# Rotary attention on one core: two half sums of a group's first numerator stack with one score between them instead of two

## The reference

```
q_rot = einsum('bhci,cij->bhcj', q, R);  k_rot = einsum('bhci,cij->bhcj', k, R)
attn_num = exp(einsum('bhqd,bhkd->bhqk', q_rot, k_rot) / scale)
attn_den = exp(einsum('bhqd,bhkd->bhqk', q, k) / scale)
attn_den = sum(attn_den, axis=-1, keepdims=True)
attn = where(causal == 0, 0.0, attn_num / attn_den)
y = einsum('bhqk,bhkd->bhqd', attn, v)
```

## Time and profile before

| | |
|---|---|
| median of 3 runs | 1891.65 us (1891.63 to 1892.13) |
| profiled execution | 1890.58 us |
| its span (first to last instruction) | 1888.6 us |
| TensorE busy | 1632.1 us (86%) |
| ScalarE busy | 1442.5 us (76%) |
| VectorE busy | 1193.2 us (63%) |
| mean granted clock of TensorE | 0.963 |

### The profile page before, as it was taken

How to read it: one execution, slowest core, us unless ns; L and a number is a source line. 1 busy time by engine, 2 the same in 40 slices (tenths; PEclk the granted TensorE clock), 3 DMA queues, 4 the chain that set the end, 5 groups by cost and what they waited for, 6 DMA issues and landing times. The chain is left out here.

```text
span 1888.6 us, 33689 instructions
## 1 busy us (share of the span) xinstructions
PE 1632.1 (86%) x12879; PEld 628.3 (33%) x12964; DVE 1193.2 (63%) x2130; ACT 1442.5 (76%) x2508; POOL 315.0 (17%) x420
## 2 busy tenths in 40 slices
PE   5799999999999999864888888989888888883995
PEld 3222222222222222241333332433343333222674
DVE  7999989999999999887454636454545423223220
ACT  4477777777777778725999999999989999991321
POOL 4500010010001001032000100010001032312466
PEclk9799999999999999977999999999999999996998
DMA  5311111111111110004111211122111222232333
GB/s 169 98 39 38 38 44 38 39 44 38 38 38 44 38 39 20 8 25 157 50 43 44 93 51 51 60 71 89 51 51 63 89 85 89 95 115 66 117 57 30
DMA packets 70960, 115.86 MB, mean 61 GB/s; under 512 B 10041, under 2 KB 55973, under 8 KB 66192
## 3 DMA queue, kind: packets, MB, share of 16 engines
q1 hardware_dynamic: 59536, 92.88, 15.6%
q0 software_dynamic: 11264, 20.83, 4.0%
HBM read 71.49 MB, written 42.14 MB: 60 GB/s over the span
## 5 line engine op out<-in xcount | busy, mean ns | idle before, releaser
L786 ACT ACTIVATE rows_and_probs<-psS 128x512 f32<-128x512 f32 x1010 | 549.1, 596 | 166.7 <-PE psS L684 166.0
L808 DVE TENSOR_REDUCE max_of_halves<-psM 128x2 f32<-128x1024 f32 x512 | 623.9, 1225 | 54.6 <-PE psM L647 20.5
L1647 ACT ACTIVATE exps<-cpsS 128x1024 bf16<-128x1024 f32 x512 | 546.3, 1109 | 22.7 <-PE cpsS L1389 22.1
L1389 PE MATMUL cpsS<-rotary_stack 128*128 128x512 bf16 x959 | 288.1, 385 | 77.6 <-ACT exps L1647 30.5
L704 PE MATMUL psO<-rows_and_probs,plain_v 128*9 128x256 f32 x4096 | 317.6, 382 | 5.3 <-ACT rows_and_probs L786 0.6
L1657 ACT ACTIVATE cprobs<-cpsS 128x1024 f32<-128x1024 f32 x256 | 281.7, 1100 | 21.6 <-PE cpsO L1422 18.9
L1369 PE MATMUL cpsS<-rotary_stack 128*128 128x512 bf16 (+3 forms) x748 | 188.5, 327 | 54.1 <-ACT exps L1647 35.5
L647 PE MATMUL psM<-plain_top 64*128 64x512 bf16 x1024 | 205.9, 384 | 20.6 <-DVE max_of_halves L808 20.2
L684 PE MATMUL psS<-plain_top 64*128 64x512 bf16 x1010 | 208.4, 388 | 0.0
L684 PE MATMUL psS<-plain_rest 64*128 64x512 bf16 x1010 | 202.6, 378 | 0.0
L1422 PE MATMUL cpsO<-cprobs,rotary_v 128*9 128x512 f32 (+3 forms) x1536 | 153.7, 488 | 0.8 <-DVE rotary_sums L1981 0.8
(11 more groups left out here) (301 smaller groups left out, 1756.1 us busy)
## 6 DMA issues: line engine op xcount, KB each, us to landing
rotary_stack<-q_parts SPq DMA_DIRECT2D x48, 192.0 KB
rotary_stack<-k_parts SPq DMA_DIRECT2D x48, 192.0 KB
rotary_stack<-q_rot_parts SPq DMA_DIRECT2D x48, 192.0 KB
rotary_stack<-k_rot_parts SPq DMA_DIRECT2D x48, 192.0 KB
tokens_taken<-parts_and_sums POOLq DMA_DIRECT2D x32, 259.0 KB, 4.2
plain_top<-q_parts SPq DMA_DIRECT2D x64, 96.0 KB
plain_top<-k_parts SPq DMA_DIRECT2D x64, 96.0 KB
e_x<-tokens_taken SPq DMA_DIRECT2D x8, 518.0 KB, 9.9
```

The lines of the kernel that those rows point to most:

```text
L786: act.activation(pr[n % SLOTS_P][:, h, :], score_bank(u), ACT.Exp, scale=SCALE).then_inc(s_e, 1)
L808: dve.tensor_reduce(mh[g % 2][cq][:, :, hh, t, kh:kh + 1].rearrange("p e o -> p (e o)"), psM[n % 2][:, :, :], AX.X, ALU.max).then_inc(s_r, 1)
L1389: ins = pe.matmul(to[:, kh, :], q[:, x, y_ * P:(y_ + 1) * P], k[:, x, kh * CH:(kh + 1) * CH], start=True, stop=True)
L1647: act.activation(ex[d % EX][:, :, :], psS[n % 3][:, :, :], ACT.Exp, scale=SCALE, accum_out=den[:, at:at + 1]).then_inc(s_e, 1)
```

## The change

In `causal_sums` the step from c0 to the next sum is 1 place instead of 2.

```
@@ -978,7 +978,7 @@
         free = max(free, seq.index(num) + 3)
         for chunk in range(2 if kind == "wide" else 1):
             at[free] = (kind, n, chunk)
-            free += 2
+            free += 1 if kind == "wide" and n == 0 and chunk == 0 else 2
     return at
```

## The result

The changed kernel takes 1881.51 us as the median of 7 runs, beside 1892.17 us for the kernel before in 7 runs. The ratio is 0.9942 with a 95% interval of 0.9931 to 0.9953, so 0.47% to 0.69% faster. In a second comparison, of five rounds, it is 0.9946 (0.9933 to 0.9959). The sign and the mechanism were forecast, the size was not: 7.4 us were forecast, and by the two ratios 10.2 to 11 us came.

What follows compares the result with a forecast made beforehand. ScalarE was taken to bound the rotary stage. Terms of 4.5 + 2.5 + 0.2 + 0.2 = 7.4 us take the median from 1891.65 to 1884.2 us, 0.39% less, with an 8-in-10 range of 1881.2 to 1888.0.

Steps and rivals of the forecast that it cites:

- What bounds the stage: Rotary stage: ScalarE, busy 792.2 of 826.6 us, is the bound; TensorE follows with slack.
- Rival A: Rotary stage: TensorE bounds, so the gain comes back a few places later; 1891.6 us, between 1889 and 1893; chance 0.14.
- rival B: Every group: lone sum ahead of score 22 costs 0.55 us against 0.45 gained, so slower, 1893.3 to 1895.7; chance 0.04.
- Term 1: Ten plain groups: c1 starts 0.45 us earlier, the wait at place 19 shrinks from 0.73 to 0.28 us; 4.5 us.
- Term 2: Groups 2, 5 and 12, fill behind place 19: 0.83 us gained each whatever the fill's length; 2.5 us.
- Term 3: Groups 4, 7 and 8: `fo` or `v` takes back most of the gain; 0.2, 0.1 and -0.06 us, together 0.2 us.
- Term 4: Work moved elsewhere, such as group 9's copy, group 10's place 1 and 44 fills: +0.2 us, bounded by -2 and +2.

Runs made afterwards that it cites:

- lone_and_plan: Against the kernel before: c0 and c1 at old places, lone sum behind place 21, VectorE's copy one place earlier, fills moved as in the change; ratio 0.9987.
- after: The changed kernel, first profile, against the kernel before: 1881.51 us beside 1892.17 us, ratio 0.9942.
- after_again: The changed kernel run and profiled a second time, against the kernel before: 1879.26 us beside 1889.17 us, ratio 0.9946.
- c1_only: Against the kernel before: only c1 moved, behind the score of place 19; lone sum, VectorE's copy and fills stay; ratio 0.9967.
- sums_old_plan: Against the kernel before: all sums and VectorE's copy moved as in the change, but the 44 fills keep their old places; ratio 0.9959.
- sums_plan_21: Against the kernel before: sums as in the change, but the planner is told 21, one place earlier still; ratio 0.9953.
- swap_c1_at_20: Against the kernel before: places 19 and 20 exchanged, sums at their old places with c1 at 20; ratio 0.9942.
- c1_at_18: Against the kernel before: c1 directly behind c0, both behind the score of place 18; lone sum, copy and fills at old places; ratio 0.9957.
- swap_old_plan: Against the kernel before: places 19 and 20 exchanged, sums at the change's new places, fills as before; ratio 0.9934.

## Why the prediction was right or wrong

**What bounds the stage: right.** ScalarE's busy time is unchanged and the stage shrank by what its idle time shrank. Rival A is refuted by the group table, rival B by lone_and_plan. The page of the Trainium skill that the prediction names (Perfetto Trace Analysis, Identifying the Most-Contended Engine) pointed the same way, and the trace agrees: with TensorE's matmuls at 86% and its weight loads at 34% of the stage, a new order of the same work made the stage 8 us shorter.

**Term 1, plain groups, 0.45 us each: right.** 0.43 to 0.46 in the profiles of after, after_again, c1_only and sums_old_plan; the wait is 0.30 us where 0.28 was forecast.

**Term 2, groups 2, 5 and 12, 0.83 us each: right in kind, too large by a fifth.** They gave 0.56, 0.68 and 0.67, 1.9 instead of 2.5 us. The step that failed is the length of the fill: I took it from rows where it stands behind a score (1.33, 0.59), and behind a sum it costs 0.11 us more (1.44 in group 2, 0.70 in group 5). Group 2 gave some of the rest back at place 32.

**Term 3, groups 4, 7 and 8, 0.2 us together: 1.0 us.** Group 4 gave 0.27 (forecast 0.2), group 8 0.12 (about 0). Group 7 gave 0.64 instead of 0.1: 0.45 with c1 alone, and 0.18 more with the lone sum and the copy (c1_only, sums_old_plan). Most of that is at place 35, which the forecast had not looked at. I had priced `v` at 1.21 us from the earlier trace rows. The score behind it is printed there as x1, one of its two matmuls: the first one's record is missing, and it had started earlier. In the changed kernel both records are there:

```profile
1263.20 1.16 PE L1489 MATMUL cpsB<-l_w,l_xt 128*128 128x128 f32 x8
1264.19 0.59 PE L1369 MATMUL cpsS<-rotary_stack 128*128 128x512 bf16 x2
```

0.99 us, and exponential 22 comes only 0.09 us later by it.

**Term 4, work moved elsewhere, +0.2 us within -2 and +2: the step that failed.** Beyond the 0.44 us of a plain group, group 9 gained 1.4 us, group 10 0.1 and group 15 1.3: 2.8 us in all, beyond the bound. The experiments give 1.05 us for the lone sum and the copy, of which group 9's copy is nearly all, and 1.98 for the fills, of which group 15 is 1.32; these 3.0 us contain the 0.2 us of group 7 that term 3 has. I had seen group 9's two waits and group 10's, and set them off against accidents of moved fills. For group 15 I had not compared the places at all, although its waits before places 32 and 42 lie in the trace of before and `fy`, `fo`, `rt` and `l` all moved. ScalarE's wait at group 10's place 1, shows that such a step can be read:

```profile
1398.66 1.02 ACT L1647 ACTIVATE exps<-cpsS 128x1024 bf16<-128x1024 f32 x1 [0.80 <-PE cpsS L1389]
```

1.83 us became 0.80, and the next place got 0.7 us new. Both the sign and the size could have been worked out group by group, with the fill's old and new place and ScalarE's wait beside it.

**The sum.** 7.2 us for terms 1 to 3 and 0.2 for term 4 were forecast; two of the ten plain groups are groups 0 and 13, so 6.5 us of it fall on the 14 groups of the table. The runs show 9.2 us there: 3.5 for term 1 (forecast 3.6), 1.9 for term 2 (2.5), 1.0 for term 3 (0.2) and 2.8 for term 4 (0.2). That terms 1 to 3 came to 6.4 us against 6.3 forecast is luck in part, since term 2 was 0.6 us too large and term 3 0.8 us too small. Term 4's 2.6 us are most of the miss, 7.4 against 10.2 to 11.0. With group 13 it is 9.7 us in the second profile; the timed gain is 10.2 and 11.0 us by the two ratios. The remaining 1 us is not settled: it is less than the interval (5 us), and group 0, group 13 and the tail vary by more than that from one execution to the next.

## What to carry to other kernels

When the engine that bounds a stage waits for a result at a fixed place, count the work that its supplier must finish before that place, and ask first whether another item can be handed to the waiting engine meanwhile: exchanging two places was worth as much (0.9942) as moving the sums and the fills was, within the intervals, and the two together 0.9927. When an edit feeds a planner, treat the moved tasks as a change of their own: list each task's old and new place beside the waits of the bounding engine, and price them one by one. And when a duration is read from the start of the next instruction, look whether that instruction has all its records. When one group of one profile stands out, look at the granted clock there before its order is blamed.

## What the runs showed of the hardware

Behind group 0, the granted clock of TensorE fell inside the stage in three of the thirteen profiles: in group 8 of sums_plan_21 and group 9 of swap_c1_at_20 (a mean of 0.66 over 5 us in each, shown with the experiments), and in group 13 of the second profile of the kernel before. Windows there (columns as in the earlier trace rows):

```profile
1557.00:1566.00 9.00, 6.15 (x31) 3.44 (x32) 2.21 (x8) 7.64 (x16) 0.83 (x3) 0.81 0.54 190
1566.00:1600.00 34.00, 28.09 (x182) 10.15 (x182) 14.34 (x84) 31.80 (x52) 8.03 (x9) 1.00 0.20 64
```

In the first profile of the kernel before the same part of group 13 ran at 1.00. Just ahead of the drop most engines paused. The rows of the second profile from 1557.8 us on, of TensorE, VectorE, GpSimd and ScalarE:

```profile
1557.85 0.60 PE L1494 MATMUL cpsB<-ident,rotary_sums 128*128 128x128 f32 x4
1558.62 0.69 DVE L1981 COPY rotary_sums<-cpsO 128x512 f32<-128x512 f32 x1 [19.82 <-remote]
1558.71 0.40 POOL L2019 COPY rotary_v<-late_values 128x256 f32<-128x256 f32 x1 [1.37 <-remote]
1558.72 1.02 ACT L1647 ACTIVATE exps<-cpsS 128x1024 bf16<-128x1024 f32 x1 [1.36 <-PE cpsS L1389]
...
1559.89 0.60 PE L1389 MATMUL cpsS<-rotary_stack 128*128 128x512 bf16 x2 [1.43 <-ACT exps L1647]
```

VectorE, GpSimd and ScalarE start again within 0.1 us of each other. ScalarE and GpSimd had done nothing for 1.4 us; VectorE's copy starts 3.7 us behind the start of its lone sum, where it is 0.7 us in the first profile. TensorE ran a score and four transposes meanwhile, and its next score follows an exponential later, after 1.43 us of idle time. What stopped the engines is not in the trace, so the cause stays open.

In each of the three cases TensorE had stood idle shortly before the clock fell, for 1.55, 1.44 and 1.43 us, and the drop began within 2 us of the end of that pause. The other ten profiles have neither a pause as long nor a drop between 905 us and the end of the stage. Whether the pause causes the drop was not tested. A mean clock of 0.66 over 5 us, or 0.81 over 9, means that part of it ran at 1.2 GHz instead of 2.4.

Group 13 is 1.76 us behind the first profile at place 3, 1.47 at place 19, and loses another 0.74 at place 42, 2.21 in all. Three more profiles have a smaller break at places 3 to 5 of this group and a loss at place 42, all at a clock of 1.00: the first of the changed kernel, c1_at_18 and swap_old_plan. So most of what it costs is not the clock. Such a break comes in some executions and not in others, in either kernel, and costs 0.7 to 2.2 us where it comes. This is why group 13 stands outside the sums of the table.
